# Context's second chunk as 64-row products in both halves of TensorE's array, three product tiles in the prologue, and VectorE's own product ahead of the sums

## What is computed

```
# windows: 8 queries x 8 keys, 16 heads of 16
attn = jnp.einsum('bhqd,bhkd->bhqk', q, k) * D ** (-0.5)
attn = softmax(attn + bias); out = jnp.einsum('bhqk,bhkd->bhqd', attn, v)
# cross-attention: context (16, 77, 192), Wk and Wv (192, 1024)
k = context @ Wk
v = context @ Wv
```

## Time and profile before

| what | us |
|---|---|
| median of 3 runs (1294.44 to 1295.89) | 1295.12 |
| the profiled execution's own time | 1294.82 |
| its span, first to last instruction | 1292.7 |
| context's keys and values on TensorE | 42.3 to 132.9 |
| windows' items on VectorE, with softmax | 45.6 to 133.9 |

### The profile page before, as it was taken

One profiled execution on the slowest core, in us unless ns is written; L12 is line 12 of the kernel. 1 busy time (PEld: TensorE's weight loads), 2 busy tenths in 40 slices (PEclk: granted clock), 3 DMA queues, 4 the chain that ended last, 5 costly groups with the idle time before them and its releaser, 6 DMA issues. The chain is left out here.

```text
span 1292.7 us, 22147 instructions
## 1 busy us (share of the span) xinstructions
PE 1184.8 (92%) x8032; PEld 976.6 (76%) x8032; DVE 850.3 (66%) x1501; ACT 596.8 (46%) x987; POOL 653.9 (51%) x541
## 2 busy tenths in 40 slices
PE   5999799999999999999999999827999999999996
PEld 2666457876677777577767777617999999999996
DVE  3688346777557776567774443437887788888883
ACT  1243423544414435324454445225666666666662
POOL 6347208466548474386484212241556455555651
PEclk9999899999999999999999999958999999999998
DMA  8433301111220111201114211035566666666650
GB/s 181 128 118 118 91 19 43 45 29 45 37 58 18 35 30 36 52 11 40 34 36 134 41 40 37 17 100 186 195 230 236 205 227 218 227 202 226 223 179 3
DMA packets 95382, 133.46 MB, mean 103 GB/s; under 512 B 42394, under 2 KB 76908, under 8 KB 89411
## 3 DMA queue, kind: packets, MB, share of 16 engines
q1 hardware_dynamic: 79299, 111.30, 27.6%
q0 software_dynamic: 16000, 21.07, 6.0%
HBM read 113.04 MB, written 24.73 MB: 107 GB/s over the span
## 5 line engine op out<-in xcount | busy, mean ns | idle before, releaser
L1777 PE MATMUL psH<-xhigh,whigh 128*128 128x256 f32 x736 | 209.1, 284 | 8.1 <-DVE wlow L1625 6.7
L1777 PE MATMUL psH<-xlow,whigh 128*128 128x256 f32 x736 | 206.7, 281 | 0.0
L1777 PE MATMUL psH<-xhigh,wlow 128*128 128x256 f32 x736 | 206.7, 281 | 0.0
L1625 DVE TENSOR_TENSOR wlow<-staged,whigh 128x2048 fp32r<-128x2048 f32 x69 | 158.6, 2300 | 0.0
L1694 ACT ACTIVATE whigh<-staged 128x2048 fp32r<-128x2048 f32 x69 | 132.3, 1919 | 54.2 <-DMA staged<-in_L_ffn_w 37.3
L1777 PEld LDWEIGHTS psH<-xhigh,whigh 128*128 128x128 f32 x736 | 141.2, 192 | 8.7 <-issue 6.9
L1777 PEld LDWEIGHTS psH<-xlow,whigh 128*128 128x128 f32 x736 | 140.0, 190 | 0.0
L1777 PEld LDWEIGHTS psH<-xhigh,wlow 128*128 128x128 f32 x736 | 139.8, 190 | 0.0
L1519 POOL TENSOR_TENSOR idle<-e_less 128x1 f32<-128x1 f32 x42 | 50.5, 1202 | 173.0 <-DMA ids_now<-ids 92.9
L1280 PE MATMUL psD<-vo,pT 128*128 128x128 f32 x1024 | 131.3, 275 | 0.1
L1280 PEld LDWEIGHTS psD<-vo,pT 128*128 128x128 f32 x1024 | 124.0, 192 | 7.9 <-issue 7.3
(11 more groups left out here) (217 smaller groups left out, 2663.7 us busy)
## 6 DMA issues: line engine op xcount, KB each, us to landing
staged<-in_L_ffn_w SPq DMA_DIRECT2D x69, 1024.0 KB, 5.0
tokens<-out_rows POOLq DMA_DIRECT2D x32, 256.0 KB, 7.3
kT<-k_cols SPq DMA_DIRECT2D x16, 308.0 KB, 2.8
vo<-v_rows SPq DMA_DIRECT2D x16, 308.0 KB
xb<-in_x SPq DMA_DIRECT2D x32, 128.0 KB
b2s<-in_L_ffn_b SPq DMA_DIRECT2D x23, 128.0 KB, 2.9
k_cols<-qT SPq DMA_DIRECT2D x4, 616.0 KB
v_rows<-pT SPq DMA_DIRECT2D x4, 616.0 KB
```

Of the source, the lines that this page charges most:

```text
L1625: tt(wlow[par][:, i, :], staged[:, i, :], whigh[par][:, i, :].bitcast(F32), ALU.subtract)\
L1777: ins = mm(psH[:, q % 2 * PAIR + c, part, :], lhs, rhs, start=i == 0, stop=i == len(passes) - 1)
```

## The change

Five things change.

1. `wk` and `wv` hold their second chunk of 64 rows twice, in partitions 0 to 63 and again in 64 to 127 (two more loads on SyncE's queue). `turn_context` writes the context's second chunk into both halves too: a transpose for rows 0 to 63, as before, and a matmul by the identity for rows 64 to 127. ScalarE copies all 308 columns at once, and GpSimd's three fills with zeros are gone.
2. `both_halves` makes two banks together: the first chunk of one and of the other with all 128 rows, then the second chunk of one with rows 0 to 63 and of the other with rows 64 to 127. `keys` uses it for K0 with K1 (three times, one block of columns each), `context_values` for both halves of a sequence. K2 has no partner: its second chunk is a product of rows 0 to 63 alone. Two banks must be free at once, and become full at once.
3. The first windows' products go to three tiles, `xw`, `tmp1` and `oT`, and a product waits for the sum three items ahead.
4. VectorE makes its product of item i before the sum of item i - 1.
5. Since `oT` is a product tile now, TensorE waits for all 16 sums before `output_turn`.

```diff
+        first_products = [xw[:], tmp1[:],
+                          oT[:].rearrange("p k b i w -> p (k b i w)").rearrange("p (i c) -> p i c", i=WS)]
...
-            eng.wait_ge(consumed, item + 1 if n == 0 else item)
+            if item > 0:
+                eng.wait_ge(consumed, item)
...
-            sp.dma_start(wk[0:CTXD - P, 1, :], Wk[P:CTXD, :]).then_inc(ctx_in, 16)
+            sp.dma_start(wk[0:D2, 1, :], Wk[P:CTXD, :]).then_inc(ctx_in, 16)
+            sp.dma_start(wk[D2:P, 1, :], Wk[P:CTXD, :]).then_inc(ctx_in, 16)
...
-            s.done(nc.gpsimd.memset(ctxT[:], 0.0))
-            s.done(nc.gpsimd.memset(wk[CTXD - P:P, 1, :], 0.0))
-            s.done(nc.gpsimd.memset(wv[CTXD - P:P, 1, :], 0.0))
...
-            for i in range(WS):
-                if i not in POOL_FIRST:
-                    make_product(dve, nc.vector.tensor_tensor, 0, i, i, False, s.done)
+            for i in range(0, WS, 2):
+                make_product(dve, nc.vector.tensor_tensor, 0, i, i, False, s.done)
+                if i > 0:
+                    sum_scores(0, i - 1)
                 sum_scores(0, i)
+            sum_scores(0, WS - 1)
...
-                    ins = nc.tensor.transpose(ps[0:CTXD - P, (2 + q) * CTX:(3 + q) * CTX], ctx[0:CTX, 2 * i + q, P:CTXD],
-                                              ident[0:CTX, 0:CTX])
+                    cols = slice((2 + q) * CTX, (3 + q) * CTX)
+                    nc.tensor.transpose(ps[0:D2, cols], ctx[0:CTX, 2 * i + q, P:CTXD], ident[0:CTX, 0:CTX])
+                    ins = mm(ps[D2:P, cols], ctx[0:CTX, 2 * i + q, P:CTXD], ident[0:CTX, 0:CTX], start=True, stop=True)
...
+            def both_halves(ps, lhs, rhs, out):
+
+                for k in range(2):
+                    mm(out(ps[k], k), lhs(0, k, slice(0, P)), rhs(0, k, slice(0, P)), start=True, stop=False)
+                for k in range(2):
+                    rows = slice(k * D2, (k + 1) * D2)
+                    yield mm(out(ps[k], k), lhs(1, k, rows), rhs(1, k, rows), start=False, stop=True)
...
+                ps = [freeA(f"K{n}.{i}", -1, -1) for n in range(2)]
+                for r in range(3):
+                    done = list(both_halves(
+                        ps, lambda c, k, rows: wk[rows, c, (3 * k + r) * P:(3 * k + r + 1) * P],
...
+                bank = freeA(f"K2.{i}", -1, -1)
+                for r, u in enumerate(range(6, CH)):
+                    for c, rows in ((0, slice(0, P)), (1, slice(0, D2))):
...
+            pe.wait_ge(consumed, 2 + TMP_ITEMS)
             for k in range(4):
                 output_turn(0, k)
```

More of the change, by code:

```diff
@@ L165, in trunk @@
         tmp1 = sb("tmp1", [P, WS, C])
-        first_products = [xw[:], tmp1[:]]
-        products = [tmp1[:], wk[:].rearrange("p k n -> p (k n)").rearrange("p (i c) -> p i c", i=WS),
-                    wv[:].rearrange("p k n -> p (k n)").rearrange("p (i c) -> p i c", i=WS)]
         idle = sb("idle", [P, 1])
@@ L180, in trunk @@
         oT = sb("oT", [P, KC, GB, WS, BLK])
+        first_products = [xw[:], tmp1[:],
+                          oT[:].rearrange("p k b i w -> p (k b i w)").rearrange("p (i c) -> p i c", i=WS)]
+        products = [tmp1[:], wk[:].rearrange("p k n -> p (k n)").rearrange("p (i c) -> p i c", i=WS),
+                    wv[:].rearrange("p k n -> p (k n)").rearrange("p (i c) -> p i c", i=WS)]
         xb = sb("xb", [P, 2, 2, C])
@@ L265, in product_of_item @@
         def product_of_item(n, i):
-            return first_products[i % 2] if n == 0 else products[(n * TMP_ITEMS + i) % 3]
+            return first_products[i % 3] if n == 0 else products[(n * TMP_ITEMS + i) % 3]
         def product_count(n, i):
@@ L320, in _ @@
             sp.dma_start(wk[:, 0, :], Wk[0:P, :]).then_inc(ctx_in, 16)
[L321 removed]
+            sp.dma_start(wk[0:D2, 1, :], Wk[P:CTXD, :]).then_inc(ctx_in, 16)
+            sp.dma_start(wk[D2:P, 1, :], Wk[P:CTXD, :]).then_inc(ctx_in, 16)
             sp.dma_start(wv[:, 0, :], Wv[0:P, :]).then_inc(ctx_in, 16)
[L323 removed]
+            sp.dma_start(wv[0:D2, 1, :], Wv[P:CTXD, :]).then_inc(ctx_in, 16)
+            sp.dma_start(wv[D2:P, 1, :], Wv[P:CTXD, :]).then_inc(ctx_in, 16)
             for key in range(WS):
@@ L630, in pair_turned @@
                 ps, value = full(f"CTX.{i}", -1, -1)
-                nc.scalar.activation(ctxT[:, i % 2, 0, :], ps[:, 0:2 * CTX], copy)
-                then(act, nc.scalar.activation(ctxT[0:CTXD - P, i % 2, 1, :], ps[0:CTXD - P, 2 * CTX:4 * CTX], copy),
+                then(act, nc.scalar.activation(ctxT[:, i % 2].rearrange("p c n -> p (c n)"), ps[:, 0:4 * CTX], copy),
                      a_done, value)
@@ L880, in _ @@
             window_divide(0)
-            for i in range(WS):
-                if i not in POOL_FIRST:
-                    make_product(dve, nc.vector.tensor_tensor, 0, WS + i, i, True, s.done)
+            for i in range(0, WS, 2):
+                make_product(dve, nc.vector.tensor_tensor, 0, WS + i, i, True, s.done)
+                if i > 0:
+                    sum_values(0, i - 1)
                 sum_values(0, i)
+            sum_values(0, WS - 1)
             start_sequence(-1, -1)
@@ L1114, in turn_context @@
                 ins.then_inc(a_full, 1)
+            def both_halves(ps, lhs, rhs, out):
[4 more added lines that the diff above has]
+                    yield mm(out(ps[k], k), lhs(1, k, rows), rhs(1, k, rows), start=False, stop=True)
             def keys(i):
                 take_a(f"CTX.{i}", -1, -1)
[L1118 to L1124, removed]
-                    ins.then_inc(a_full, 1)
@@ L1127, in context_values @@
-            def context_values(i):
[L1128 to L1134, removed]
+                ps = [freeA(f"K{n}.{i}", -1, -1) for n in range(2)]
@@ new lines, in keys @@
+                for r in range(3):
+                    done = list(both_halves(
+                        ps, lambda c, k, rows: wk[rows, c, (3 * k + r) * P:(3 * k + r + 1) * P],
+                        lambda c, k, rows: ctxT[rows, i % 2, c, :],
+                        lambda bank, k: bank[:, r * 2 * CTX:(r + 1) * 2 * CTX]))
+                for ins in done:
+                    ins.then_inc(a_full, 1)
+                bank = freeA(f"K2.{i}", -1, -1)
+                for r, u in enumerate(range(6, CH)):
+                    for c, rows in ((0, slice(0, P)), (1, slice(0, D2))):
+                        ins = mm(bank[:, r * 2 * CTX:(r + 1) * 2 * CTX], wk[rows, c, u * P:(u + 1) * P],
+                                 ctxT[rows, i % 2, c, :], start=c == 0, stop=c == KC - 1)
@@ new lines, in keys @@
+                ins.then_inc(a_full, 1)
+            def context_values(i):
+                for q in range(2):
+                    ps = [freeA(f"V{2 * q + half}.{i}", -1, -1) for half in range(2)]
+                    for ins in list(both_halves(
+                            ps, lambda c, k, rows: ctxT[rows, i % 2, c, q * CTX:(q + 1) * CTX],
+                            lambda c, k, rows: wv[rows, c, k * 512:(k + 1) * 512],
+                            lambda bank, k: bank[0:CTX, :])):
+                        ins.then_inc(a_full, 1)
@@ L1177, in _ @@
             pe.wait_ge(constants, 3)
-            pe.wait_ge(ctx_in, 16 * 5)
+            pe.wait_ge(ctx_in, 16 * 7)
             turn_context(0)
```

## The result

| | us |
|---|---|
| changed kernel, median of 6 runs (1299.38 to 1302.10) | 1301.13 |
| kernel before on the same chip, median of 6 runs (1292.90 to 1296.54) | 1294.78 |
| ratio, with its 95% interval | 1.0048 [1.0035, 1.0061] |
| the changed kernel's profiled execution | 1302.02 |

The change costs 6.4 us by the medians (6.2 by the ratio; 4.5 to 7.9 by its interval). The direction was forecast, and the time lies in the range; the forecast sum was 8.8.

The account below looks back on a forecast made before the run. The prediction took TensorE's end in the prologue as the bound: 0.8 (keys, values) + 5.3 (context turns) + 1.4 (front) + 0.7 (bank stall) + 0.6 (last copy) = 8.8 on 1294.8, giving 1303.6 us, whole range 1298 to 1307.

Parts of the forecast that it names:

- The excursion, 0.31 to 0.40: TensorE going to 64-row products and back: 0.31 us with 77-column weights, 0.40 for keys with 128 columns.
- The identity product, bounds 0.13 and 0.44: Each added product in `turn_context`: 0.13 us for records only, 0.44 with an excursion; 0.44 taken, +5.3 over six turns.
- rival A: The identity product in `turn_context` costs its records only: sum 5.0, time 1299.8 us; chance 0.22.
- Keys and values, +0.10 a pair: TensorE per pair: values -1.10 us, keys +1.20, together +0.10, or +0.8 in all.
- The last pair has none ahead of it, and stalls by 0.9 - 0.15 = +0.7: Before the last pair's keys, no context turn covers TensorE's wait for V2's bank: +0.7 us.
- The front, "+1.4": Two context turns ahead of the first keys add 1.78 us less a 0.36 wait for ScalarE: +1.4.
- the tail: After TensorE's last value product, V3's bank is emptied one 0.59 us copy later, delaying store and `oT`: +0.6.
- VectorE's branch: VectorE's last sum in the prologue ends at 134.4 against TensorE's 141.1, so its gains are worth nothing.
- The same granted clock behind the prologue: TensorE's granted clock, 0.81 over 132.9 to 160 us before the change, was taken unchanged after it.
- B: Excursions on TensorE are cheap, below 0.25 us each, so the change is faster; 1287 us if free; chance 0.08.
- D: The 64-row halves do not overlap on TensorE: 2.5 us more a pair, 20 in all, 1324 us; chance 0.04.
- C: A draw: excursions near 0.25 us, or growth in front and at banks overlapped; 1294 to 1297 us; chance 0.09.

Follow-up runs that it names:

- kernel 1: TensorE's part of the change alone, VectorE and GpSimd code, tiles and wait as in the kernel before: 1298.29 us, ratio 1.0052 to the kernel before.
- kernel 3: The changed kernel with 128-row and 64-row chunks in alternating order, so 64-row products stand together: 1292.68 us, ratio 0.9994 to the kernel before.
- kernel 4: The changed kernel without the identity product, ScalarE copying the context's second chunk into both halves: 1297.73 us, ratio 1.0041 to the kernel before.
- kernel 2: The kernel before with VectorE's part alone (three product tiles, new order, wait for all sums): 1291.82 us, ratio 0.9992 to the kernel before.
- kernel 6: The changed kernel with keys at full height and ScalarE copying the half instead of the identity product: 1286.32 us, ratio 0.9940 to the kernel before.
- kernel 7: kernel 6 with the second sequence's 64-row value products first, next to the first sequence's: 1282.82 us, ratio 0.9907 to the kernel before.
- kernel 8: kernel 7 with the wait for weights behind the score items and `Exp` behind the fourth pair's keys: 1283.53 us, ratio 0.9912 to the kernel before.
- kernel 9: kernel 8 with sequence 0's keys and values loaded once the first pair is stored: 1281.94 us, ratio 0.9908 to the kernel before.
- kernel 5: The changed kernel with keys made at full height as before, values in halves and identity product kept: 1292.16 us, ratio 0.9983 to the kernel before.

## Why the prediction came out as it did

**The mechanism was right.** What follows TensorE's end sets the start of the trunk, that end comes later by the changes of form, and what it loses reaches the trunk whole. Kernels 1 and 3 show each half of it.

**The excursion, 0.31 to 0.40.** Confirmed: 0.37 from kernel 3, as a mean. By the starts above, eight key records with one excursion take 56.52 - 55.34 = 1.18 us, for 0.53 + 0.265 of work: 0.39. Eight value records take 63.61 - 60.72 = 2.89, for 1.72 + 0.86: 0.31. Both are the sizes that the forecast used. TensorE's timeline of the changed kernel, in windows so narrow that single records stand apart, shows where it goes:

```profile
54.34 0.23 PE L1117 MATMUL psA<-ident,ctx 77*64 77x77 f32 x1
54.50 0.28 PE L1118 MATMUL psA<-ident,ctx 77*64 77x77 f32 x1
54.62 0.23 PE L1118 MATMUL psA<-ident,ctx 77*64 77x77 f32 x1
54.78 0.28 PE L1115 MATMUL psA<-ident,ctx 77*128 77x77 f32 x1
...
57.02 0.29 PE L1124 MATMUL psA<-ctxT,wk 128*128 128x154 f32 x1
57.25 0.40 PE L1127 MATMUL psA<-ctxT,wk 64*128 64x154 f32 x2
```

57.02 to 57.25 is 0.23, of which 0.13 are the record's own: 0.10 to go over, close to the 0.09 of the earlier trace rows in the trunk. The Trainium skill (TensorEngine Tiling (Array Packing), Key Properties) has the drain at a change of mode; the records here agree, with 0.10 us on the way over. The way back is not separated here from the weight load.

**The identity product, bounds 0.13 and 0.44.** It stands between 54.34 and 54.78: the record ahead takes 0.16 for its 0.067 of work, the product's two take 0.12 and 0.16. The turn grew by 0.85 for two, 0.42 each. The upper bound was the right one, and rival A falls: this product, which writes partitions 64 to 127 alone, is as dear as one that reads 64 rows. Six turns made +5.1, forecast +5.3.

**Keys and values, +0.10 a pair.** Measured 11.16 against 11.11: +0.05, in eight pairs +0.4 for +0.8.

**Terms that were mis-sized.** "The last pair has none ahead of it, and stalls by 0.9 - 0.15 = +0.7": there is no stall. The last pair's keys start at 127.95, while ScalarE copies V2's bank only from 128.11. I had taken the bank order of the other pairs. Without a context bank of its own the last pair shifts by one bank, and K0 and K1 take V0's and V1's, both empty. That is 0.7 of the 2.5 us by which the forecast was too high (8.8 - 6.35). The front, "+1.4", measured 2.19 - 1.06 = +1.13 from the first context product to the first keys. That product came 0.41 sooner than in the profile of before (40.87 for 41.28); over all eleven profiles it stands between 40.85 and 42.23, so that is scatter and not the change's. Together the front is off by 0.7. With 0.4 for keys and values, 0.2 for the turns and 0.1 for the tail, the misses make 8.8 - 6.8 = 2.0, and `norm2` is 6.8 later. The rest down to 6.4 is within the measurement.

**VectorE's branch.** Forecast end 134.4, measured 133.18; the errors in it partly cancel. The first product came 3.5 us later, not 2.2; in kernels 1, 3 and 4, with the same two loads, it came at 47.49 to 47.79, 1.9 to 2.2 us later, so the 2.2 was sound and the rest is this profile's. From there to the shifted scores it took 34.2 us instead of 43.0: 8.8 saved, not 6.4. I had counted the three later periods and left out the first, in which VectorE's product takes 2.29 (49.14) instead of 6.60 and its next one 4.17 (53.79) instead of 2.29: 2.4 us more. `Exp` came 4.0 later instead of 5.0. Values saved 4.7, forecast 4.5. That none of it matters, with some 6 us of cover, is what kernel 2 shows, and kernel 1, where the cover is 1.4 us and the ratio (1.0052) that of the changed kernel within the noise.

**The same granted clock behind the prologue.** It did not hold in this profile. The stretch starts with the output turns, as the second row does to within 0.05 us, and is as long to within 0.05 us; columns as there.

```profile
139.11:166.26 27.15, 18.32 (x76) 13.96 (x74) 4.56 (x12) 11.65 (x28) 3.85 (x6) 0.75 0.38 109
```

The clock is 0.75 instead of 0.81, and the first query products take 6.62 us (154.16 to 160.78) instead of 5.22. Both kernels start them at a granted clock of 0.50, the lower of its two levels (1.2 GHz). In the kernel before, the first three stretches of 2 us from their start (147.37) have 0.50, 0.65 and 1.00; in the changed one (from 154.16) 0.50, 0.50 and 0.50. That is some 1.3 us of full-speed work less in those 6 us, about the 1.4 us by which they are longer. Whether the change does this is open: see the last section.

**Rivals.** B, a cheap excursion, is refuted at nine excursions a pair; its mechanism still pays where records are long and excursions few, as kernels 6 and 7 show. D is refuted: 64-row records of 512 columns that accumulate onto 128-row products run two at a time. C, a draw, is what kernel 3 gives: at six excursions a pair the change is worth nothing either way.

## What to carry to other kernels

Price a change between 128-row and 64-row products by how often the form changes, 0.3 to 0.4 us for each excursion here, and not by record times alone: two halves of 512 columns save 0.86 us for one excursion and win, two of 154 columns save 0.265 and lose. Where it is used, order the products so that those of one form stand next to one another, and let something else than a product fill the second half. When a branch has been shortened, look for the next one each time: here TensorE, then VectorE and the round trip through DRAM within 0.1 us of each other, then the round trip alone set the end, and an edit that was worth nothing came to be needed, by the estimate at kernel 7.

## What the runs showed of the hardware

- **A product onto partitions 64 to 127 alone costs as much as a change of form.** The identity product uses all 77 of its rows, but only the columns for partitions 64 to 127, between transposes onto 128 and onto 64 columns. Those transposes change among themselves without a gap (0.067 us each); the product costs 0.42 us for 0.13 of records. It is also the only matmul among transposes; the keys' first matmul follows the last transpose without a gap before the change (53.78 in the earlier trace rows), so that alone is unlikely to be it, but no run separates the two.
- **ScalarE carries data across partitions.** It reads partitions 0 to 63 of PSUM and writes 64 to 127 of SBUF in the copy itself (kernels 4 and 6 to 9). In kernel 4 that copy, 64 x 154 fp32, takes 0.29 us, and the same copy to partitions 0 to 63 takes 0.28.
- **VectorE's and GpSimd's products exclude each other both ways.** For the scores the prediction had GpSimd waiting for VectorE. GpSimd's first product in the changed kernel, in its timeline,

```profile
49.15 6.66 POOL L290 TENSOR_TENSOR tmp<-staged 128x2048 f32<-128x2048 f32 x1 [23.17 <-DMA rb_b<-in_L_ffn_router_b]
```

  ends at 55.81, and VectorE's product that started inside it, at 53.79, ends at 57.96: 2.15 after it, about its own 2.29. The later one waits, whichever it is. The Trainium skill (SBUF — State Buffer, Who interferes with whom) says that a VectorE instruction with two SBUF inputs contends with a GpSimd instruction that reads SBUF, and that the order of issue decides which one blocks; the rows agree. Each meeting of two such products thus costs the later one about the overlap: VectorE 1.9 us here (4.17 for 2.29) and 4.3 in the kernel before (6.60 for 2.29, where GpSimd's product had started 0.06 earlier, at 45.56, and took 4.51), and GpSimd 2.1 in the other direction (6.56 for 4.51).
- **The first products behind the prologue scatter, with the granted clock.** The first 16 query records take 5.34 to 6.78 us in the profiles of the eleven kernels: 5.39 before and in kernel 1, 6.78 after, 6.66 in kernel 5, 5.35 in kernel 9. They stand behind 12 to 15 us in which TensorE mostly waits for the other engines, and start at a granted clock of 0.50 in all eleven. Their length follows the clock: in the third 2 us from their start it is 1.00 where they take 5.39 (before), 0.89 where they take 5.90 (kernel 6), 0.73 where they take 6.22 (kernel 4) and 0.50 where they take 6.78 (changed). When the clock comes back does not follow the edits in any order that I could see, and sets a floor of about 1.5 us under what two single profiles can tell.
